# Layer 0 of a graph network: lookups, products, gathers and scans moved into one stage

## The chip, the cores and the metric

The kernel runs on one core of a Trainium2 chip. A core has TensorE (PE), VectorE (DVE), ScalarE (ACT), GpSimd (POOL) and SyncE (SP); each takes its instructions in order and they wait for each other on semaphores. The metric is the time of one execution on the device in microseconds (us), the median of several; lower is better.

## The reference

3125 nodes of 768 features pass through a two-layer graph attention network (GAT) and a mixture-of-experts network. Only layer 0 of the GAT is touched:

```python
h = (x @ W).reshape(n, heads, out_c)             # x layer-normed; 8 heads of 96
al_s = einsum('nhc,hc->nh', h, a_src)
al_d = einsum('nhc,hc->nh', h, a_dst)
e = leaky_relu(al_s[src] + al_d[dst], 0.2)       # 50000 edges, sorted by dst
m = segment_max(e, dst)
ex = exp(e - m[dst])
z = segment_sum(ex, dst)
out = segment_sum(h[src] * (ex / z[dst])[:, :, None], dst) + bias
```

## The kernel before

Nodes are padded to 25 blocks of 128 (`NB`), edges to 392 tiles of 128 (`NT`). The program is a row of parts, `run(setup)`, `run(features)`, `run(transform)`, `run(scores)`, `run(aggregate)`, and then layer 1 (`features_next`, `products_scores`, ...) and the experts. Each part has a block of its own; the next begins when all engines have finished it. Within a part the order on each engine is the order of the code.

`features` (L284) first makes the attention weights `wa` (12 pairs of a product and a reduction on VectorE, L256 and L257), then handles the 25 blocks: statistics and normalising on VectorE (L331 to L340), six transposes (L352) and six small matmuls for the scores (L360) on TensorE, the square root and two copies (L385, L387) on ScalarE. It ends by storing the table `score_tab`.

`transform` (L533) has 28 turns of 14 edge tiles. Of each turn, 6 tiles' source scores are looked up on TensorE: the low seven bits of `src` are broadcast by a matmul (L653), compared with the partition number (`picks`, L756), the one-hot picks rows of the table by matmul (`lookup`, L662; the table stands in three bf16 parts), and VectorE masks the block and sums (`masked`, L761 to L770). The other 8 tiles are gathered by GpSimd from `score_tab` (L722), up to four turns ahead (`AHEAD`), by indices that VectorE copies to `islot` (L775). Each turn also counts, for the node of each edge, with one-hots of `dst` (`hots`, L792, and L670); the counts give each node's first edge, `first_idx`. The first 25 turns each carry the products of one block (L679, one accumulator), whose rows ScalarE copies and stores to `feat_tab`. The first 12 turns carry the weights of layer 1 as well.

`scores` (L895) scatters each node's `al_d` to the place of its first edge (25 indirect DMAs, L909), reads that array back, and scans: a forward maximum, a backward maximum and the spread of the first values. Each is eight scans, a carry through TensorE, and eight scans again (L955, L966, L968). Five passes over 3136 elements, the exponential, a trip through memory and 32 transposes (L934) give the edge weights.

`products_scores` of layer 1 (L984) does all this for one head in one stage; there every score is looked up, in groups of 8 tiles with the low bits read back from memory (`lo_rows`), and GpSimd has the scatters alone (L1032).

## Time and profile before

| | |
|---|---|
| median of 3 runs | 2875.5 us (2863.57 to 2877.48) |
| the profiled execution's own time | 2895.24 us |
| its span in the trace | 2893.3 us |
| mean granted clock of TensorE | 0.764 |
| busy: TensorE, VectorE, ScalarE, GpSimd | 62%, 45%, 28%, 45% |
| `features` ends, `transform` ends, `scores` ends | 111.5, 523, 629.8 us |

The rows below are of that one execution. L679 is line 679 of the kernel before. A row of a timeline gives the start and the length in us, the engine, the line, the operation with what it writes and reads, and in brackets how long the engine was idle before it and whose work ended the wait; "issue" means that the profile shows nothing it waited for. A row of a group gives the busy time, the mean length in ns, and the idle time before its instructions.

### The profile page before, as it was taken

To read this page: it belongs to the slowest core of one execution; us is meant where nothing else is said; L and a number is where in the kernel's file an instruction comes from. 1 tells how busy PE (TensorE), PEld (TensorE's weight loads), DVE (VectorE), ACT (ScalarE), POOL (GpSimd) and SP (SyncE) were. 2 spreads that over 40 slices of the span, in tenths; PEclk is the share of its full clock that TensorE was granted. 3 is DMA by queue.
4 is the path that set the end of the run, shared out by engine and by line. 5 is a ranking of instruction groups with operands and counts; after the bars stand their busy time and mean duration, and the time that the engine had idled before them with its cause. 6 is when DMAs were issued, how large, how long until landed. Compare 5 with 4: busy or idle time off the path is not lost. (4 is left out here: it accounts for less than half of the span.)

```text
span 2893.3 us, 47710 instructions
## 1 busy us (share of the span) xinstructions
PE 1802.4 (62%) x15107; PEld 1191.7 (41%) x15108; DVE 1307.3 (45%) x2560; ACT 797.7 (28%) x2189; POOL 1309.7 (45%) x1277
## 2 busy tenths in 40 slices
PE   3678888125645555566567955555555568899970
PEld 2445554013333333334334533333333346677750
DVE  7646655655655566548367124111111125311116
ACT  3301111013323333344222323333333332233320
POOL 0266755426767676760221136666666610111216
PEclk9789889556666766758789976676676677899995
DMA  4311111037777787765389698999889874344559
GB/s 142 106 35 41 37 35 30 24 106 248 253 238 251 250 253 252 253 209 176 92 215 261 177 258 288 314 310 316 307 311 317 307 255 150 110 164 156 165 170 400
DMA packets 178077, 577.27 MB, mean 200 GB/s; under 512 B 40579, under 2 KB 49794, under 8 KB 177752
## 3 DMA queue, kind: packets, MB, share of 16 engines
q0 software_dynamic: 88208, 373.59, 42.2%
q1 hardware_dynamic: 64462, 133.66, 13.6%
q10 hardware_dynamic: 25344, 69.32, 6.2%
q8 instruction: 23, 0.38, 0.1%
q14 instruction: 40, 0.33, 0.0%
HBM read 473.58 MB, written 96.45 MB: 197 GB/s over the span
## 5 line engine op out<-in xcount | busy, mean ns | idle before, releaser
L722 POOL DMA_INDIRECT work<-score_tab,islot x224 | 235.3, 1050 | 143.7 <-DVE islot L775 75.8
L1314 POOL DMA_INDIRECT ring<-feat_tab,islot x196 | 234.9, 1198 | 88.3 <-issue 51.6
L1378 PE MATMUL acc<-ring,work 128*32 128x192 f32 x1952 | 179.6, 479 | 127.2 <-issue 67.4
L1572 PE MATMUL acc<-ring,work 128*32 128x192 f32 (+1 forms) x1952 | 171.3, 477 | 139.4 <-issue 106.8
L679 PE MATMUL acc<-wg,work 128*128 128x384 f32 x600 | 227.9, 529 | 28.7 <-issue 24.7
L1494 POOL DMA_INDIRECT ring<-feat_tab,src_t x196 | 195.7, 998 | 108.8 <-PE acc L1572 54.0
L1120 PE MATMUL acc<-wg,work 128*128 128x384 f32 x600 | 215.7, 509 | 19.2 <-ACT work L1177 19.2
L1351 DVE TENSOR_TENSOR ring<-ring,edges 128x768 f32<-128x768 f32 x196 | 185.3, 960 | 89.6 <-DMA ring<-feat_tab,islot 76.8
L1382 PEld LDWEIGHTS acc<-edges,work 128*32 128x32 f32 x982 | 148.2, 152 | 100.9 <-issue 4.7
L679 PEld LDWEIGHTS acc<-wg,work 128*128 128x128 f32 x600 | 120.6, 206 | 122.1 <-issue 59.7
L1572 PEld LDWEIGHTS acc<-ring,work 128*32 128x32 f32 x1952 | 87.3, 144 | 202.3 <-issue 179.9
L1378 PE MATMUL acc<-work 128*32 128x192 f32 x1104 | 99.0, 438 | 106.6 <-ACT work L1436 49.4
L2019 POOL COPY tile_idx<-wg 128x3 int32 x19 | 4.6, 244 | 338.4 <-PE tps L2032 224.5
L1314 POOL DMA_INDIRECT work<-feat_tab,islot x112 | 127.9, 1142 | 56.0 <-issue 27.2
L1572 PE MATMUL acc<-work 128*32 128x192 f32 x1104 | 100.4, 484 | 81.0 <-issue 69.9
L1120 PEld LDWEIGHTS acc<-wg,work 128*128 128x128 f32 x600 | 113.6, 197 | 87.4 <-ACT work L1177 19.3
L1440 ACT ACTIVATE work<-work 32x192 f32<-32x192 f32 x400 | 143.8, 360 | 5.3
L1650 ACT ACTIVATE work<-work 32x192 f32<-32x192 f32 x400 | 143.8, 359 | 5.3
L1494 POOL DMA_INDIRECT work<-feat_tab,src_t x112 | 108.2, 966 | 62.3 <-PE acc L1572 31.1
L2140 DVE TENSOR_TENSOR edges<-acc,wg 128x192 f32<-128x192 f32 x57 | 20.4, 358 | 251.8 <-PE acc L2040 235.7
L1382 PE MATMUL acc<-edges,work 128*32 x982 | 122.7, 198 | 2.3 <-issue 2.2
L2040 PE MATMUL acc<-big,work 128*128 x684 | 122.1, 329 | 1.0 <-ACT work L2096 1.0
(383 smaller groups left out, 3742.2 us busy)
## 6 DMA issues: line engine op xcount, KB each, us to landing
slot_out<-ring SPq DMA_DIRECT2D x57, 384.0 KB
feat_tab<-work ACTq DMA_DIRECT2D x50, 384.0 KB
ring<-lo_rows SPq DMA_DIRECT2D x49, 256.0 KB, 5.8
edges<-in_w_slow SPq DMA_DIRECT2D x28, 384.0 KB, 9.9
edges<-in_w_hebb POOLq DMA_DIRECT2D x28, 384.0 KB, 7.9
edges<-in_w_fast POOLq DMA_DIRECT2D x28, 384.0 KB, 9.4
unit_sum<-edges SPq DMA_DIRECT2D x28, 384.0 KB, 7.0
agg_raw<-work ACTq DMA_DIRECT2D x25, 388.0 KB
```

What stands on the lines that cost most here:

```text
L679: m = nc.tensor.matmul(acc[:, sl * 2 + c, 0:C // 2], xT[sl][:, k, :], wg[:, k, c * (C // 2):(c + 1) * (C // 2)], start=(k == 0), stop=(k = ...
L722: pool.indirect_dma_start(sg[:, h, k * H:(k + 1) * H], None, score_tab[0], bass.IndirectOffsetOnAxis(ap=islot[:, h * 8 + k:h * 8 + k + 1], ...
L1120: m = nc.tensor.matmul(acc[:, sl * 2 + c, 0:C // 2], xT[sl][:, k, :], wg[:, k, c * (C // 2):(c + 1) * (C // 2)], start=(k == 0), stop=(k = ...
L1314: pool.indirect_dma_start(rows[k][:, 0:C], None, feat_tab[l], bass.IndirectOffsetOnAxis(ap=islot[:, h * UN + k:h * UN + k + 1], axis=0)).t ...
L1351: V.tensor_tensor(r3, r3, ex[:, ds(i * UN + k, 1), :].rearrange("p a h -> p h a").to_broadcast([P, H, C // H]), ALU.mult).then_inc(msg_rea ...
L1378: m = nc.tensor.matmul(sums_ps[c * WIN:(c + 1) * WIN, 0:CHUNK], hot, row[:, c * CHUNK:(c + 1) * CHUNK], start=start, stop=True, skip_group ...
L1382: return nc.tensor.matmul(sums_ps[0:WIN, CHUNK:CHUNK + ZC], hot, ex[:, ds(t, 1), :].rearrange("p a h -> p (a h)"), start=False, stop=True, ...
L1440: nc.scalar.activation(raw[sl][w * WIN:(w + 1) * WIN, c * CHUNK:(c + 1) * CHUNK], stage[w % 2][c * WIN:(c + 1) * WIN, 0:CHUNK], ACT.Copy)
L1494: pool.indirect_dma_start(rows[k][:, 0:C], None, feat_tab[1], bass.IndirectOffsetOnAxis(ap=src_t[:, t:t + 1], axis=0)).then_inc(row_in[k], 16)
L1572: m = nc.tensor.matmul(sums_ps[c * WIN:(c + 1) * WIN, 0:n], hot, row[:, c * CHUNK:c * CHUNK + n], start=start, stop=True, skip_group_check ...
L1650: nc.scalar.activation(raw[b % 2][w * WIN:(w + 1) * WIN, c * CHUNK:(c + 1) * CHUNK], stage[w % 2][c * WIN:(c + 1) * WIN, 0:CHUNK], ACT.Copy)
L2040: m = nc.tensor.matmul(acc[:, 2, 0:HID], xTs[k][:, c, :], big[:, ds(e * HID + c * EH, HID)], start=(c == 0), stop=(c == KC - 1))
```

## The change

`features` is written out over the blocks. x is loaded ahead of W0; VectorE starts the statistics at once and makes `wa` in blocks 3 to 8; ScalarE normalises (with a new `shift`), and one copy of the transposed block instead of two is made. The index work of `transform` moves here. A node's first edge is now found so: the last edge's `dst` of each tile (`dst_last`) is counted per node, which gives the tile in which the node's edges begin (`tiles_of_nodes`); GpSimd gathers that tile's row of `dst_rows` for each node (25 gathers), and VectorE compares it with the node's number (`compared`).

`products_scores_first` takes the place of `transform` and `scores`. It has the form of layer 1's stage: 56 groups of 4 tiles (224 tiles) are looked up on TensorE, four groups between the product chunks of a block, two accumulators; GpSimd sends the 25 scatters and then gathers 168 tiles, with a wait for the lookups at every eighth; the scan of the first values comes after group 48, the two others after the last gather; products of the last blocks stand between.

```diff
+GF = 4
+FIRST_GROUPS = (LOOK_BLOCKS + 2) * GPB
+LOOKED = FIRST_GROUPS * GF
+PACE = 8
...
+                    def compared(g):
+
+                        dve.wait_ge(near_in[g], 16 * SB)
+                        for j in range(SB):
+                            b = g * SB + j
+                            V.tensor_scalar(less[:, j, :], near[:, b, :].bitcast(i32), node_f[:, b:b + 1], None, ALU.is_lt)
+                            ins = V.tensor_scalar(same[:, j, :], near[:, b, :].bitcast(i32), node_f[:, b:b + 1], None, ALU.is_equal)
+                        st.step(ins)
+                        V.tensor_reduce(below_n[:, g * SB:(g + 1) * SB], less, AX, ALU.add)
+                        st.step(V.tensor_reduce(miss[:, g * SB:(g + 1) * SB], same, AX, ALU.max))
...
+                    for b in range(NB):
+                        statistics(b)
+                        if b > 0:
+                            shifts(b - 1)
...
+                        if 3 <= b < 3 + KC:
+                            for j in range(2):
+                                attention_weights(st, 0, b - 3, j, wg[:, b - 3, :], a_vec[j], wa_tmp)
...
+                @block.gpsimd
+                def _(pool):
...
+                    for b in range(NB):
+                        pool.indirect_dma_start(first_val[0], bass.IndirectOffsetOnAxis(ap=first_idx[:, b:b + 1], axis=0),
+                                                al_node[:, b, H:2 * H], None, bounds_check=EP - 1,
+                                                oob_is_err=False).then_inc(first_st, 16)
+                    for t in range(LOOKED, NT):
+                        n = t - LOOKED
+                        if n % PACE == 0:
+                            pool.wait_ge(look_ps, max(1, n * FIRST_GROUPS // (NT - LOOKED) - 2))
+                        pool.indirect_dma_start(src_s[:, t, :], None, score_tab[0],
+                                                bass.IndirectOffsetOnAxis(ap=src_p[:, t:t + 1], axis=0)).then_inc(gather_in, 16)
...
+                    def lookup(G, j):
+                        pe.wait_ge(pick_ready, G + 1)
+                        pe.wait_ge(look_used, G + 1)
+                        for c in range(GF):
+                            for part in range(3):
+                                m = nc.tensor.matmul(look[j][:, c // 2, (c % 2) * W:(c % 2 + 1) * W],
+                                                     pick[j][:, c * P:(c + 1) * P], table[:, part, :],
+                                                     start=(part == 0), stop=(part == 2))
+                        m.then_inc(look_ps, 1)
...
+                    steps = {(LOOK_BLOCKS, 5): lambda: carry_out(0, dst_s[:, NT - 1, :]),
+                             (LOOK_BLOCKS + 1, 1): lambda: carry_back(0, 2),
+                             (FB + 1, 0): lambda: carry_out(1, peak[:, NT - 1, :]),
+                             (FB + 1, 1): lambda: carry_back(1, 0),
+                             (FB + 3, 1): lambda: carry_out(2, top[:, 0, :]),
+                             (FB + 3, 2): lambda: carry_back(2, 1),
+                             (NB - 1, 0): lambda: weights_out(0),
...
+                    with dve.Fori(0, KC // 2) as i:
+                        st.loop(i, 2 * (LO * 3 + 4))
+                        for s in range(2):
+                            for g in range(LO):
+                                picks((i * 2 + s) * LO + (g + 1), (g + 1) % 2, (g + 1) % LO, i * 2 + (s + (g + 1) // LO))
+                                masked((i * 2 + s) * LO + g, g % 2)
+                            next_attention(i * 2 + s, s, i)
+                    st.done(KC // 2)
...
+                    dve.wait_ge(first_in, 16)
+                    whole_scan(0, 2, dst_s, first_s, keep, held, False, 0.0)
+                    for G in range(KC * LO, FIRST_GROUPS):
+                        if G + 1 < FIRST_GROUPS:
+                            picks(G + 1, (G + 1) % 2, (G + 1) % LO, (G + 1) // LO)
+                        masked(G, G % 2)
+                    dve.wait_ge(gather_in, 16 * (NT - LOOKED))
+                    whole_scan(1, 0, peak, src_s, rst_f, most, False, NEG)
+                    whole_scan(2, 1, top, peak, rst_b, most, True, NEG)
...
         run(setup)
         run(features)
-        run(transform)
-        run(scores)
+        run(products_scores_first)
         run(aggregate)
```

## Rows read from the trace of the kernel before

**Rows 1.** Busy time by stage (us, instructions), then granted clock, DMA share, GB/s.
```profile
111.50:523.00 411.50, 311.87 (x1674) 192.96 (x1674) 248.15 (x361) 40.20 (x75) 237.87 (x230) 0.84 0.17 42
523.00:629.80 106.80, 8.49 (x38) 5.77 (x38) 62.56 (x60) 10.60 (x10) 32.06 (x25) 0.50 0.14 46
```

**Rows 2.** Waits in 140 to 520: total us, times, longest.
```profile
POOL work L722 <- DVE islot L775: 66.9, 10, 11.7
DVE edges L766 <- remote: 60.6, 12, 14.8
```

**Rows 3.** Timeline, gathers of `transform`: start, length, instruction, idle before.
```profile
122.25 1.09 POOL L722 DMA_INDIRECT work<-score_tab,islot  x1 [8.85 <-DVE islot L775]
...
491.40 0.95 POOL L722 DMA_INDIRECT work<-score_tab,islot  x1 [0.30 <-issue]
```

**Rows 4.** Timeline, ScalarE's slot copies, one a turn.
```profile
186.17 0.84 ACT L617 ACTIVATE work<-big 128x768 f32 x1 [29.31 <-PE acc L679]
...
336.77 0.84 ACT L617 ACTIVATE work<-big 128x768 f32 x1 [8.57 <-PE acc L679]
...
366.75 0.84 ACT L617 ACTIVATE work<-big 128x768 f32 x1 [28.38 <-remote]
```

**Rows 5.** Timeline, `products_scores` of layer 1 during its scatters.
```profile
1437.51 0.85 DVE L1245 TENSOR_TENSOR edges<-tps,edges 128x300 f32<-128x300 f32 x2 [7.66 <-DMA big<-feat_tab,islot]
...
1454.48 0.97 POOL L1032 DMA_INDIRECT first_val<-al_node,first_idx  x1 [0.31 <-issue]
...
1459.30 0.85 DVE L1245 TENSOR_TENSOR edges<-mps,edges 128x300 f32<-128x300 f32 x2 [18.98 <-DMA big<-feat_tab,islot]
```

**Rows 6.** Timeline, `features` and the head of `transform`.
```profile
15.44 0.96 DVE L256 TENSOR_TENSOR edges<-wg,edges 128x768 f32<-128x768 f32 x1 [15.30 <-DMA edges<-in_a_dst]
...
39.31 0.56 DVE L331 BATCH_NORM_STATS2 stats<-ring 128x6 f32<-128x384 f32 x1
...
98.03 0.68 DVE L340 TENSOR_SCALAR work<-ring,carry 128x768 f32<-128x768 f32 x1
...
107.24 0.39 SPq L313 DMA_DIRECT2D score_tab<-al_node  x1
...
111.50 0.33 DVE L736 CAST edges<-al_node 128x200 bf16<-128x200 f32 x1 [12.79 <-PEq L300]
...
121.40 0.36 DVE L798 TENSOR_SCALAR keep<-keep 128x392 int32<-128x392 int32 x1
...
130.72 0.35 DVE L828 TENSOR_SCALAR edges<-edges 128x392 int32<-128x392 int32 x1
```

**Rows 7.** Groups of VectorE in `transform`: busy us, mean ns, idle before.
```profile
L770 DVE TENSOR_REDUCE edges<-edges 128x1200 f32 (+1 forms) x28 | 39.3, 1403 | 6.4 <-DVE edges L766 4.7 <-issue 1.5
...
L766 DVE TENSOR_TENSOR edges<-acc,edges 128x400 f32<-128x400 f32 x56 | 32.2, 575 | 47.5 <-remote 35.9 <-DVE edges L766 6.3 <-PE acc L662 2.6
```

**Rows 8.** Timeline, one group of lookups in layer 1's `products_scores`.
```profile
1582.51 0.48 DVE L1236 TENSOR_SCALAR edges<-ring,edges 128x1024 bf16<-128x1024 bf16 x1 [0.18 <-DVE edges L1250]
...
1583.51 0.85 DVE L1245 TENSOR_TENSOR edges<-mps,edges 128x300 f32<-128x300 f32 x2 [0.23 <-PE tps L1109]
...
1585.55 0.49 DVE L1236 TENSOR_SCALAR edges<-ring,edges 128x1024 bf16<-128x1024 bf16 x1 [0.18 <-DVE edges L1250]
```

**Rows 9.** Timeline, the second half of `scores`.
```profile
571.65 7.04 DVE L955 TENSOR_TENSOR_SCAN edges<-keep,edges 128x392 f32<-128x392 f32 x8 [16.34 <-DMA edges<-first_val]
...
587.74 3.42 DVE L975 TENSOR_TENSOR edges<-edges 128x3136 f32<-128x3136 f32 x1
...
621.21 0.43 PE L934 MATMUL tps<-ident,ring 98*128 98x98 f32 x1 [41.26 <-DMA ring<-edge_ex]
...
629.77 0.17 DVE L1336 COPY islot<-src_t 128x14 int32<-128x14 int32 x1 [24.77 <-PEq L905]
```

**Rows 10.** The page's group of the products.
```profile
L679 PE MATMUL acc<-wg,work 128*128 128x384 f32 x600 | 227.9, 529 | 28.7 <-issue 24.7
```

**Rows 11.** Timeline, one of the products' weight loads.
```profile
256.82 0.34 PEld L679 LDWEIGHTS acc<-wg,work 128*128 128x128 f32 x1 [0.30 <-issue]
```

850 lines of the change are left out of this document (417 added, 433 removed).

## The prediction

> **What bounds the kernel now.** I read three things in this order: the busy time by stage, who waited for whom inside the first of the touched stages, and then single instructions at the stage borders. The stages `transform` and `scores` take 411.5 and 106.8 us, 518.3 together; with `features` (to 111.5) that is 629.8 us of the span of 2893.3 [rows 1]. No engine is full in either: in `transform` TensorE is busy 312 of 411.5 us at a granted clock of 0.84, VectorE 248, GpSimd 238; in `scores` VectorE is busy 62.6 of 106.8 and TensorE 8.5 [rows 1]. So the second stage is a chain on one engine, and the first is something that holds three engines together.
>
> What holds them shows in the waits. GpSimd waited 66.9 us for `islot`, which VectorE fills after each turn, and VectorE waited 60.6 us in `masked` for a releaser that the profile calls "remote", which is none of the engines' finished work [rows 2]. GpSimd's own pace is 0.95 + 0.30 = 1.25 us a gather, so 224 gathers need 280 us; from the first at 122.25 to the end of the last at 492.35 it took 370 [rows 3]. 90 us were lost, 0.40 us a gather. Much of it sits in a few stretches: one turn on ScalarE, at best some 10 us (8.57 of them idle), lasted from 336.77 to 366.75, 30 us, and one like it ended at 186.17 [rows 4]. Layer 1 shows the same without gathers: in `products_scores` VectorE stood 7.66 and 18.98 us before two multiplications while GpSimd sent its 25 scatters, and went on at 1459.30, after the last scatter at 1454.48 [rows 5]. I call this the standstill: engines with long instruction streams stop while GpSimd sends small indirect DMAs back to back, and go on when it pauses. Why, the trace doesn't say.
>
> **The change, part by part.** I place S, the start of the new stage (before: 111.5), then T, when VectorE has all scores of sources, then the tail.
>
> *features, to S.* Before, VectorE first made the attention weights, 15.44 to 39.31, 23.9 us, and only then the first statistics; 25 blocks follow to 98.03, 2.35 us each, and the score table is stored at 107.24 [rows 6]. After, x comes first, so statistics can begin near 7 us (the first load is issued a little after 4 us; my guess from the store-to-next-stage distance of 107.24 to 111.50, which bounds a small DMA and a stage border by 4.3 us [rows 6]). But VectorE gets much more. The normalising (0.68 us) goes to ScalarE, which drops its second copy of each block for it; with the new shift (0.15) what is left is about 1.8 us a block, 45 us for 25. Added: weights 23.9; what was the head of `transform`, 121.40 to 130.72, 9.3 us [rows 6]; `compared`, 5 groups of ten 128-wide comparisons and two reductions over 640, by the reduction's rate (1.403 us for 1200, [rows 7]) 0.75 each and 0.2 a comparison (one of 392 elements takes 0.36 [rows 6]), 3.5 to 3.7 us a group, 18.4; histogram, small copies and index sums, 6. Sum 7 + 45 + 23.9 + 9.3 + 18.4 + 6 = 110, plus some 5 us of waits for W0, which now stands behind nine loads in SP's queue and is wanted at block 3. Then the last block runs through the pipeline (normalise, six transposes, copy, six matmuls, two copies) in about 5 us (before 9.2, 98.03 to 107.24, with three blocks under way), and 4.3 to the next stage as before. S = 124; 118 if the waits vanish, 134 if 25 new gathers of rows in this stage cost 0.40 us each as above. The stage gets 12 us longer.
>
> *Lookups, S to T, on VectorE.* Removed: the counting one-hots, the broadcast through PSUM, the index copies and the waits for gathers. Left are 56 groups of 4 tiles. Layer 1 does the same with 8 narrower tiles: 1582.51 to 1585.55, 3.04 us a group [rows 8]. Here the pick has 512 instead of 1024 elements (less 0.2), the mask 100 instead of 200 (less 0.1), the multiplications are two of 400 instead of 300 (0.575 and 0.50 pipelined against 0.85, plus 0.2 [rows 7, 8]), the reduction has 800 instead of 600 (0.95 by the rate above, plus 0.2). 3.15 us, and 56 of them 176. The weights of layer 1, the same 12 pairs as in `features`, 24. The first-value scan, now between groups 48 and 49, 571.65 to 587.74 before, 16.1 [rows 9]. Start 4. Sum 220.
>
> *Gathers, on GpSimd.* 25 scatters and 168 gathers at 1.25 to 1.28: 247, 251 with start and landing. This is longer than 220, so without the standstill T = S + 251, and VectorE has 31 us to spare. With it VectorE's time grows. The scatters meet the first lookups as in layer 1: 7.66 + 18.98 = 27 us [rows 5]. The gathers: 90 x 168/224 = 67 if the price of before holds, 0 at best. Against 67 speaks the new wait: at every eighth gather GpSimd stops until the lookups are near, where before it could run four turns (32 gathers) ahead. The two longest stretches of before, about 20 us each too long (both in [rows 4]), could then not last. (90 - 40) x 168/224 = 37. I take 27 + 37: T = S + 284, and GpSimd, held by the same checks, ends beside it. Behind the checks nothing else waits on GpSimd's queue.
>
> TensorE: 12 products a block, 0.529 us each in the mean of before [rows 10], and 48 small matmuls, about 11 us against 14.8 on VectorE (four groups and half a pair of weights). It is no bound at this clock; at 1.2 GHz throughout, with 0.64 a product [rows 11] and the small ones twice as long, it would be about 17, 2 us a block over VectorE, some 20 us more at most. The double accumulators take ScalarE's copy off its path, worth nothing here.
>
> *Tail from T.* Two scans of 16.1; each carry now stands behind product chunks in TensorE's order, 2 us in all. The five passes, the exponential, and its way out to memory and back, 587.74 to 621.21, 33.5 [rows 9]. Then the transposes: before 8.5 us to the next stage, at 629.77 [rows 9]. Now six sit between the twelve products of the last block, which at the lower clock (1.2 GHz) come every 0.30 + 0.34 us [rows 11], 7.7, and that block's store must land: 8.5 + 7.7 + 2. Sum 32.2 + 2 + 33.5 + 18.2 = 86; 75 if the products hide. Where the 106.8 us of `scores` went: 32.4 of them, the wait for the scatters (16.34) and the scan of first values, are now inside S to T [rows 9].
>
> **Sum.** 124 + 284 + 86 = 494 against 629.8: 136 us less. Profiled execution 2895.2 (span 2893.3) gives 2759. The median shown, 2875.5, lies 19.7 below the profiled one; I subtract from it: 2740. Later stages get the same tables and indices and should keep their lengths.
>
> **A rule weighed.** VectorE's picks are bf16 from SBUF to SBUF; in layer 1 they take 0.48 us for 1024 elements, twice what one element a cycle of the 1200-wide reduction gives [rows 7, 8], while the scatters beside them stay at 0.97 [rows 5]. The Trainium skill (SBUF — State Buffer, Who interferes with whom) says that such `tensor_scalar` modes take the port pair that GpSimd shares, and the other side blocks fully. By that rule GpSimd would lose at most 56 x 0.24 = 13 us, an estimate of mine; GpSimd's 251 would become 264, still under 284. The rows here show no such loss.
>
> A second rule gives a rival of its own: the Trainium skill (Runtime: NRT & Kernel Launch, Instruction fetch mechanics) says that a taken branch outside the fetched window stalls its engine.
>
> **Rivals.**
> - *No standstill*, chance 0.22: the loops, not the indirect DMAs, cause it, and they shrink (TensorE's from 27 turns to 6, VectorE's from 6 to 3, ScalarE's from 12 to none). For: gathers stayed at 0.95 during it. Against: layer 1 stood in mid-body, and as long as the scatters ran [rows 5]. T = S + 251, 33 less than forecast: 2707. This is also what the rule just named would give.
> - *Full price*, 0.22: pauses don't help. 27 + 67: T = S + 314: 2770.
> - *The other side*, 0.04: between two checks the engines stand entirely and lookups advance only in the pauses. 21 checks x 8 x 1.25 = 210 us instead of 37: 2740 + 173 = 2913, slower. For: that one turn of 30 us [rows 4]. Against: the gathers of 28 turns took 370 us, 13.2 a turn [rows 3], so most went beside running engines. It decides from 173 us lost in the gathers up, 8 us a check.
> - *features is the surprise*, 0.04: VectorE's order there stalls on SP's queue or the near gathers; 30 us more, 2770.
>
> **Chances.** Forecast 0.48. Its own range 2715 to 2765. Of the range I leave out the far side and a small rest: 2707 less 30 for a short tail and S = 118 gives 2677; 2770 plus 10 for S = 134 and 15 to 20 for the lower clock 2795 to 2800. So 2675 to 2800. A measurement of this kernel tells some 0.5%, 14 us. Faster 0.93, same 0.03, slower 0.04.
>
> **What would show it.** Right: score table stored near 120; 56 groups about 3.15 us apart where GpSimd pauses; VectorE gaps of some 27 us within the first 35 us of the stage; gathers ending within 10 us of the last lookup; the five passes ending near 460; `aggregate` starting near 494. Wrong: `features` over 135; VectorE waiting long for the last gathers (no standstill); a period above 5 us a group; or the last block's products starting after the transposes and adding more than 10 us.

## The result, and the profile after

The changed kernel takes 2801.2 us (median of 4 runs, 2798.4 to 2805.7) against 2869.5 for the kernel before beside it (2862.3 to 2877.5): a ratio of 0.9763, 95% interval 0.9727 to 0.9798. That is 68 us faster. The forecast was 136 faster, 2740, with a range to 2800: the direction held, the size was halved, and the time lies just outside the range.

The three stages, in the view of busy time by window of the changed kernel (columns as in [rows 1]; the cuts are the start of the new stage, the first scan over the source scores, and the first instruction of `aggregate`):

```profile
0.00:145.44 145.44, 74.16 (x491) 57.10 (x492) 93.53 (x286) 53.37 (x102) 30.93 (x53) 0.97 0.39 126
145.44:480.73 335.29, 225.91 (x1067) 144.95 (x1068) 185.77 (x330) 29.04 (x50) 189.92 (x194) 0.81 0.23 57
480.73:563.72 82.99, 73.58 (x244) 43.48 (x242) 47.40 (x42) 24.57 (x35) 0.00 (x0) 0.98 0.22 82
```

S is 145.4 (forecast 124), S to T 335.3 (284), the tail 83.0 (86). The three stages end at 563.7 against 629.8 [rows 1], 66 us less. A second profile of the kernel before (below) has them end at 627.7. What follows takes 2232.9 us after and 2232.1 in that second profile, so the change left it alone; the profile on which the forecast stood had 2263.5 there and was 30 us long in stages that the change doesn't touch. The forecast's stages were 69.7 us short. It carried 10.9 us of the other sign from that profile: those 30.6 us too many in the later stages, against 19.7 that it took off for the median. With 2.8 us between the new profiled execution and its median that gives the miss of 61 us. By stage it is +21.4 in S, +51.3 from S to T and -3.0 in the tail.

**features.** The timeline of the changed kernel, TensorE, VectorE and the DMA queue of SyncE, first the steady blocks, then the end:

```profile
85.26 2.78 PE L544 MATMUL tps<-big,wa 128*16 128x128 f32 x24 [1.14 <-ACT edges L602]
...
90.20 2.78 PE L544 MATMUL tps<-big,wa 128*16 128x128 f32 x24 [1.14 <-ACT edges L602]
...
95.15 2.78 PE L544 MATMUL tps<-big,wa 128*16 128x128 f32 x24 [1.14 <-ACT edges L602]
...
99.08 0.26 DVE L522 COPY dst_open<-mps 128x100 f32<-128x100 f32 x1 [9.48 <-PE mps L571]
...
128.22 0.16 DVE L415 SCALAR_TENSOR_TENSOR carry<-carry 128x1 f32<-128x1 f32 x1
...
140.62 0.38 SPq L369 DMA_DIRECT2D score_tab<-al_node  x1
...
145.44 0.33 DVE L942 CAST edges<-al_node 128x200 bf16<-128x200 f32 x1 [16.52 <-PEq L337]
```

Three blocks start their node scores 4.94 and 4.95 us apart, each after 1.14 us idle for L602, ScalarE's copy of scores. VectorE itself, which would need less, stood 9.48 us for a transpose that TensorE had queued behind them, and made its last `shift` at 128.2, where the forecast's sum has it at some 115. From its last `shift` to the store of the score table it took 12.4 us, not 5.

**The standstill.** TensorE, GpSimd and VectorE at the head of the new stage:

```profile
166.78 0.95 PE L834 MATMUL mps<-edges 128*128 128x200 bf16 x9 [0.75 <-DVE edges L955]
168.69 0.25 PE L834 MATMUL mps<-edges 128*128 128x200 bf16 x1 [0.96 <-issue]
170.79 0.25 PE L834 MATMUL mps<-edges 128*128 128x200 bf16 x1 [1.85 <-issue]
...
174.99 0.80 PE L846 MATMUL acc<-wg,work 128*128 128x384 f32 x1 [1.77 <-issue]
177.79 0.80 PE L846 MATMUL acc<-wg,work 128*128 128x384 f32 x1 [2.00 <-issue]
...
176.36 0.97 POOL L789 DMA_INDIRECT first_val<-al_node,first_idx  x1 [0.30 <-issue]
...
178.91 1.00 POOL L796 DMA_INDIRECT edges<-score_tab,src_p  x1 [0.30 <-issue]
...
204.51 1.05 DVE L964 TENSOR_TENSOR edges<-tps,edges 128x400 f32<-128x400 f32 x2 [37.62 <-remote]
```

TensorE has no wait that the profile can name, and yet gets one lookup matmul each 2.1 us and then one product each 1.4 to 2.8 us, while GpSimd sends its scatters and, from 178.91, 16 gathers without a pause. VectorE stands 37.62 us for that one group of lookups ("remote" is again a releaser that the profile cannot name). Its waits of this kind over the stage, and GpSimd's for the lookups:

```profile
DVE edges L964 <- remote: 90.7, 15, 37.6
...
POOL edges L796 <- PE tps L834: 56.1, 7, 20.6
```

**Undisturbed groups and the tail**, in VectorE's and TensorE's timeline:

```profile
401.48 0.35 DVE L955 TENSOR_SCALAR edges<-ring,edges 128x512 bf16<-128x512 bf16 x1 [0.18 <-DVE edges L969]
...
404.70 0.35 DVE L955 TENSOR_SCALAR edges<-ring,edges 128x512 bf16<-128x512 bf16 x1 [0.18 <-DVE edges L969]
...
480.73 7.04 DVE L992 TENSOR_TENSOR_SCAN edges<-rst_f,edges 128x392 f32<-128x392 f32 x8
...
547.95 0.92 PE L869 MATMUL tps<-ident,ring 98*128 98x98 f32 x4 [4.35 <-DMA ring<-edge_ex]
...
563.72 0.17 DVE L1379 COPY islot<-src_t 128x14 int32<-128x14 int32 x1 [31.76 <-PEq L783]
```

A group takes 3.22 us where nothing disturbs it. At T there is no wait for the last gathers (480.73 follows the last group at once), and the six transposes stand between products, as drawn in the forecast.

### The profile page after: what moved, and what is told of

The parts are those of the page before. It is cut to its first block and busy times, and to the rows that moved or that the text cites. A ratio compares the mean times of both kernels' runs of the same rounds, so it can differ in the third digit from the quotient of the medians.

```text
span 2796.6 us, 46260 instructions
## 1 busy us (share of the span) xinstructions
PE 1790.1 (64%) x14721; PEld 1192.4 (43%) x14722; DVE 1246.9 (45%) x2621; ACT 807.3 (29%) x2189; POOL 1255.4 (45%) x1248
## 5 line engine op out<-in xcount | busy, mean ns | idle before, releaser
L1163 PE MATMUL acc<-wg,work 128*128 128x384 f32 x600 | 215.3, 508 | 21.4 <-ACT work L1220 18.7
L796 POOL DMA_INDIRECT edges<-score_tab,src_p x168 | 165.2, 983 | 127.2 <-PE tps L834 56.1
L1615 PEld LDWEIGHTS acc<-ring,work 128*32 128x32 f32 x1952 | 89.7, 149 | 180.3 <-issue 165.4
L2062 POOL COPY tile_idx<-wg 128x3 int32 x19 | 3.9, 207 | 335.3 <-PE tps L2075 221.1
L1615 PE MATMUL acc<-work 128*32 128x192 f32 x1104 | 96.2, 462 | 87.1 <-issue 54.7
L1421 PEld LDWEIGHTS acc<-ring,work 128*32 128x32 f32 x1952 | 58.0, 135 | 173.7 <-issue 156.7
```

The source lines that it names most:

```text
L796: pool.indirect_dma_start(src_s[:, t, :], None, score_tab[0], bass.IndirectOffsetOnAxis(ap=src_p[:, t:t + 1], axis=0)).then_inc(gather_in, 16)
L1163: m = nc.tensor.matmul(acc[:, sl * 2 + c, 0:C // 2], xT[sl][:, k, :], wg[:, k, c * (C // 2):(c + 1) * (C // 2)], start=(k == 0), stop=(k = ...
L1421: m = nc.tensor.matmul(sums_ps[c * WIN:(c + 1) * WIN, 0:CHUNK], hot, row[:, c * CHUNK:(c + 1) * CHUNK], start=start, stop=True, skip_group ...
L1615: m = nc.tensor.matmul(sums_ps[c * WIN:(c + 1) * WIN, 0:n], hot, row[:, c * CHUNK:c * CHUNK + n], start=start, stop=True, skip_group_check ...
```

## The experiments

The runs were made in seven groups, each on one chip and with the kernel before beside them; in the table, rows with the same time of the kernel before are one group. The groups are of two kinds: in four the kernel before takes 2868 to 2904 us, in three 2602 to 2608. I call them the slow and the quick chip, but only for short: the record numbers the chips of six groups, and number 9 stands for a slow group (the b-runs) and for a quick one (e2 and e3). So what makes the difference need not be the chip itself. The changed kernel's first run was in a slow group. All edits are to the changed kernel. The changed kernel itself was run in two groups only, both slow, with stretches of 335.3 and 337.7 us; kernels of other groups are compared with these.

| run | chip (before) | ratio, 95% interval | S | S to T |
|---|---|---|---|---|
| changed kernel | 2869.5 | 0.9763, 0.9727 to 0.9798 | 145.4 | 335.3 |
| a1_no_small | 2608.0 | 0.9687, 0.9637 to 0.9736 | 144.5 | 240.2 |
| a2_no_scatters | 2608.0 | 0.9655, 0.9618 to 0.9692 | 144.6 | 243.4 |
| a3_straight | 2608.0 | 0.9747, 0.9695 to 0.9799 | 145.2 | 255.4 |
| a4_copy_first | 2608.0 | 0.9716, 0.9678 to 0.9754 | 133.8 | 256.9 |
| b2_kernel_changed | 2868.4 | 0.9763, 0.9735 to 0.9791 | 144.2 | 337.7 |
| b3_combined | 2868.4 | 0.9689, 0.9665 to 0.9713 | 134.2 | 322.4 |
| b4_no_small_again | 2868.4 | 0.9434, 0.9407 to 0.9460 | 143.3 | 239.9 |
| c1_no_scatters_again | 2891.4 | 0.9659, 0.9631 to 0.9688 | 144.1 | 305.4 |
| c2_straight_again | 2891.4 | 0.9724, 0.9692 to 0.9756 | 145.5 | 329.3 |
| c3_paced | 2891.4 | 0.9744, 0.9717 to 0.9772 | 142.8 | 324.1 |
| c4_combined_64 | 2891.4 | 0.9715, 0.9676 to 0.9754 | 134.5 | 336.7 |
| d1_paced_60 | 2601.6 | 0.9715, 0.9674 to 0.9755 | 133.8 | 255.2 |
| d2_unpaced | 2601.6 | 0.9805, 0.9753 to 0.9858 | 144.4 | 254.7 |
| d3_combined_again | 2601.6 | 0.9683, 0.9645 to 0.9720 | 133.8 | 247.7 |
| e1_unpaced_again | 2903.6 | 1.0202, 1.0159 to 1.0245 | 146.4 | 477.3 |
| e2_paced_60_again | 2603.1 | 0.9698, 0.9648 to 0.9748 | 134.0 | 255.4 |
| e3_paced_60_looser | 2603.1 | 0.9703, 0.9655 to 0.9752 | 132.1 | 253.0 |

### GpSimd's small DMAs left out

```diff
-                    for b in range(NB):
-                        pool.indirect_dma_start(first_val[0], ...)
-                    for t in range(LOOKED, NT):
-                        ...
+                    nc.gpsimd.memset(src_s[:, LOOKED:NT, :], 0.0).then_inc(gather_in, 16)
...
-                            sp.wait_ge(first_st, 16 * NB)
...
-                    dve.wait_ge(gather_in, 16 * (NT - LOOKED))
+                    dve.wait_ge(gather_in, 16)
```

The first run:

> The changed kernel with GpSimd's 25 scatters of first values and 168 gathers of scores left out (the scores of those tiles are set to 0 once, the first values stay 0). Theory A, the standstill comes from GpSimd's small indirect DMAs sent back to back: VectorE's waits of kind remote and issue in its 56 groups (88 us in the changed kernel, the longest 37.6) all but vanish, and the stretch from the new stage's start to the last group shrinks from 335 us to about 56 x 3.2 + 24 + 20 = 223 to 250 us, the kernel from 2801 to about 2700 to 2715 us. Theory B, the engines stop at the taken branches of their own loops or for long instruction streams alone: the waits stay near 80 us, the stretch near 330, the kernel at about 2800. Theory C, the first 37.6 us are the collision of instruction fetches with the stage's opening loads (8 rows of low bits, four of 384 KB): these 37.6 stay and the later 50 go, the kernel is at about 2750.

It fell on a quick chip (2526.6 us), and there nothing could be told apart: the stretch was 240.2 us as theory A says, but the kernels beside it that keep their gathers had no remote wait either. The same kernel on a slow chip:

> The kernel of the first experiment again (no scatters and no gathers on GpSimd in the new stage; those scores are 0). On a chip like that of the first experiment (before at 2608): ratio to the kernel before 0.965 to 0.972 and a stretch of 240 us, as there. On a chip where the kernel before takes 2870: theory A (the standstill is called by GpSimd's small DMAs) says the stretch is 240 to 250 us and the kernel 85 to 95 us under the changed one, at 2705 to 2720; theory B (it comes of loops, of long streams or of that chip's memory alone) says the remote waits stay and the stretch is 300 us or more.

The median was 2708.6 us and the stretch 239.9 against 337.7 in the changed kernel beside it. Not one wait of kind remote is left. VectorE's longest single wait in the stage is now that for the attention vectors, and the longest for TensorE's lookups is small:

```profile
DVE edges L945 <- DMA work<-in_a_dst: 8.1, 1, 8.1
...
DVE edges L954 <- PE tps L824: 1.2, 2, 0.6
```

Theory A is shown for the slow chip: small indirect DMAs on GpSimd's queue cost TensorE and VectorE 98 us of this stage. Theory B falls, since this kernel keeps every loop. So does C, since it keeps the opening loads. The windows 180 to 220 put it side by side. With no small DMAs:

```profile
180.00:220.00 40.00, 30.12 (x163) 20.88 (x162) 31.88 (x55) 3.44 (x6) 0.00 (x0) 0.92 0.23 77
```

and in the changed kernel on the same chip:

```profile
180.00:220.00 40.00, 10.56 (x32) 5.77 (x33) 7.13 (x13) 1.72 (x3) 21.00 (x23) 0.50 0.09 19
```

163 matmuls against 32, and a granted clock of 0.92 (mostly the upper of its two levels, 2.4 GHz) against 0.50 (the lower, 1.2 GHz): TensorE, which had all but stood, was at the lower clock as well.

### The scatters alone

```diff
-                    for b in range(NB):
-                        pool.indirect_dma_start(first_val[0], ...)
...
-                            sp.wait_ge(first_st, 16 * NB)
```

> The changed kernel with only the 25 scatters left out (the first values stay 0); all 168 gathers are sent. Theory A with every small DMA alike: the stretch falls by the scatters' share of the standstill, 25 x 1.27 = 32 us of GpSimd's 200, so the 37.6 us wait shrinks to 5 to 15 us and the kernel is 20 to 33 us faster than the changed one, at about 2770 to 2780. Theory A with the gathers as the cause: the first burst of gathers (16 before the first pause) takes the scatters' place, the wait stays at 25 us or more, kernel at about 2790 to 2800. Theory B (loops or streams alone): nothing changes.

> The changed kernel without the 25 scatters of first values (those stay 0), all 168 gathers sent, meant for a chip like that of the changed kernel's first run (the kernel before at 2870). There the standstill costs 337.7 - 239.9 = 98 us of the stretch with all 193 small DMAs. If each DMA calls its share by its time on GpSimd (scatters 32 of 197 us), the stretch is about 321 and the kernel 2785 to 2792. If the scatters' unbroken run behind the stage's start is what costs (VectorE's first remote wait, 38.3 us), the stretch is about 300 and the kernel 2760 to 2772. If the first 16 gathers take the scatters' place: 330 or more, 2795 to 2805. On a chip where the kernel before takes 2608 nothing new: 243 us and a ratio of 0.966.

On the quick chip the stretch was 243.4 us (2518.4 us in all). On the slow one 305.4, 32 less than with scatters (337.7, from the b-runs, as is the 239.9 below); the first long wait is gone (the longest remote one is 11.9 us), 60.3 us of remote waits remain. That is nearest to the second case: the ratio of 0.9659 would be 2770 us where the kernel before takes 2868. The scatters, first part of the unbroken run behind the stage's start, cost about one for one, 32 us of sending and 32 us of standstill. The 168 gathers alone still cost 305.4 - 239.9 = 65.5 us, 0.39 us each.

### No pause at all

```diff
-                        if n % PACE == 0:
-                            pool.wait_ge(look_ps, max(1, n * FIRST_GROUPS // (NT - LOOKED) - 2))
+                        if n == 0:
+                            pool.wait_ge(look_ps, 1)
```

> The changed kernel with no pause between GpSimd's gathers (one wait for the first group, then 168 in a row after the 25 scatters). If TensorE gets only a matmul or so per 0.7 to 2.1 us while GpSimd sends without a pause, it stands for most of 25 x 1.27 + 168 x 1.25 = 242 us, in which some 60 to 100 matmuls (3 to 5 groups) get through, and 51 groups follow undisturbed at 3.2: a stretch of 242 + 51 x 3.2 + 44 = about 450 us, and a kernel about 110 us slower than the changed one, at 2910 (ratio 1.01 to 1.02) where the kernel before takes 2870 to 2890. If each DMA costs the same 98 / 193 = 0.5 us of standstill whatever the spacing, the stretch is 330 to 345 us and the ratio 0.976. Where the kernel before takes 2608 nothing changes in either.

> The unpaced kernel again (168 gathers in a row behind the 25 scatters), for a chip on which the kernel before takes 2870 to 2890; its first run fell on one with 2602, where the stretch took 254.7 us against the changed kernel's 257 or so and told nothing of the standstill. Price by the unbroken run: a stretch of about 450 us and a ratio of 1.01 to 1.02. Price per DMA whatever the spacing: 330 to 345 us and 0.976.

On the quick chip: 254.7 us, set by GpSimd (VectorE waited 11.7 for the last gather). On the slow chip the same kernel is 2% slower than the kernel before (interval 1.6% to 2.4%), 2964.7 us, and the stretch is 477.3. VectorE's and GpSimd's timeline there:

```profile
219.04 1.06 DVE L964 TENSOR_TENSOR edges<-tps,edges 128x400 f32<-128x400 f32 x2 [50.73 <-remote]
...
263.84 1.06 DVE L964 TENSOR_TENSOR edges<-mps,edges 128x400 f32<-128x400 f32 x2 [41.81 <-remote]
...
319.84 1.06 DVE L964 TENSOR_TENSOR edges<-tps,edges 128x400 f32<-128x400 f32 x2 [53.01 <-remote]
...
364.67 1.06 DVE L964 TENSOR_TENSOR edges<-mps,edges 128x400 f32<-128x400 f32 x2 [41.84 <-issue]
...
415.79 1.06 DVE L964 TENSOR_TENSOR edges<-tps,edges 128x400 f32<-128x400 f32 x2 [48.09 <-remote]
...
391.13 0.94 POOL L796 DMA_INDIRECT edges<-score_tab,src_p  x1 [0.30 <-issue]
```

One group of lookups each 45 to 56 us, until the last gather has been sent at 392.1. In the windows:

```profile
220.00:260.00 40.00, 6.01 (x16) 2.60 (x16) 1.60 (x4) 0.00 (x0) 30.25 (x33) 0.50 0.08 7
...
440.00:480.00 40.00, 34.96 (x200) 24.40 (x199) 31.74 (x59) 3.75 (x7) 0.00 (x0) 0.96 0.34 106
```

16 matmuls in 40 us while GpSimd sends, 200 after, the clock 0.50 and then 0.96. GpSimd sent for 244 us and the stretch grew by 477.3 - 239.9 = 237: at full length of run the engines all but stand. The number of DMAs is that of the changed kernel, which lost 98. So the price is not one per DMA; it hangs on the pauses.

### Paced from the first one

```diff
                     for b in range(NB):
+                        if b % 3 == 0:
+                            pool.wait_ge(look_ps, b // 3 + 1)
...
-                        if n % PACE == 0:
-                            pool.wait_ge(look_ps, max(1, n * FIRST_GROUPS // (NT - LOOKED) - 2))
+                        if n % 4 == 0:
+                            pool.wait_ge(look_ps, 9 + n * (FIRST_GROUPS - 9) // (NT - LOOKED))
```

> The changed kernel with all 193 small DMAs of GpSimd tied to the lookups from the first one on: one wait for the next group before every third scatter and before every fourth gather, so that GpSimd is never more than one group ahead (in the changed kernel it sends 25 scatters and 16 gathers without a pause). GpSimd's own time then gives at least 3.8 us a group for the first nine and 3.5 us for the other 47, so 200 to 205 us plus 24 + 20 + 9, at least about 255. If unbroken runs cause the standstill and a short pause lets the streams in, the first remote wait of 38.3 us goes to under 8 and the stretch falls from 337.7 to 270 to 310 us, the kernel to 2740 to 2775 where the kernel before takes 2870. If each DMA costs its share whatever the spacing, the stretch stays within 10 us of 337.7 or grows. On a chip where the kernel before takes 2608 there is no standstill to save: the stretch goes from 257 to 260 to 270, ratio 0.977 to 0.98.

The longest remote wait fell from 38.3 to 8.2 us, and the time to the end of group 48 and the weights from 290.5 to 262.9 us, but the whole stretch only to 324.1, 14 us less where 28 to 68 had been forecast. It fits neither case, and in the kernel's time the gain is not clear of the noise (0.9744 against 0.9763, the intervals overlap). The end shows why:

```profile
427.45 0.94 POOL L798 DMA_INDIRECT edges<-score_tab,src_p  x1 [24.41 <-PE tps L836]
...
444.66 1.06 DVE L966 TENSOR_TENSOR edges<-mps,edges 128x400 f32<-128x400 f32 x2 [5.66 <-remote]
...
461.94 1.06 DVE L966 TENSOR_TENSOR edges<-tps,edges 128x400 f32<-128x400 f32 x2 [8.21 <-remote]
```

GpSimd, tied to the lookups, stood through the scans of first values; then it sent its last gathers nearly in a row, and the last eight groups had the waits of 5.66 and 8.21 us. Up to group 48 this kernel still lost 68 us against the one without small DMAs (262.9 against 195.1, there 143.3 to 338.4): short pauses take off some of the price, not most. The schedule that spreads the gathers better, in the combined kernel:

```diff
-                        if n % PACE == 0: ...
+                        if n < 100 and n % 3 == 0:
+                            pool.wait_ge(look_ps, 9 + n * 39 // 100)
+                        if n >= 120 and n % 3 == 0:
+                            pool.wait_ge(look_ps, 48 + (n - 120) * 3 // 8)
```

> The combined kernel (scores' copy first, moved wait, 60 groups, 152 gathers) with GpSimd's DMAs paced from the first one on: a wait for one more group before every third scatter, then before every third of the first 100 gathers (so that they spread over groups 9 to 48), no wait for the next 20 (they go while VectorE makes the scans of first values), and again one for every third of the last 32. In the kernel paced before, the time to the end of group 48 fell by 27.6 us against the changed kernel, and 14 us were given back in the last 8 groups, where GpSimd, held still for 24.4 us during the scans, sent 32 gathers in a row. If unbroken runs set the price, this kernel keeps both: against the combined one's 322.4 us a stretch of 295 to 310, and a ratio to the kernel before of 0.958 to 0.966 where that takes 2870 to 2890. If each DMA sets it: within 0.003 of the combined one's ratio (0.969).

> The paced kernel with 60 groups again, for a chip on which the kernel before takes 2870 to 2900. The unpaced kernel has shown that the price goes by the unbroken run. If short pauses from the first DMA on then save what is left of the first run (a first wait of 16.7 and one of 23.6 us in the combined kernel), the stretch is 295 to 312 against the combined one's 322.4, and the ratio 0.958 to 0.966. If the streams need more than a short pause, the stretch is within 8 us of 322 and the ratio 0.967 to 0.972.

> The same with each wait of a gather one group earlier (two groups in the last 32), so that the gathers end some 5 us sooner. Where the kernel before takes 2870 to 2900: if a tighter tie to the lookups is what feeds the streams, 2 to 8 us slower than the tight one; if the end of the gathers holds the scans, 2 to 7 us faster. Where it takes 2602 (no standstill): the wait for the gathers of 7.7 us falls to 3 or so, and the kernel comes within 5 us of the combined one.

All three were in quick groups, where there is nothing to win back: stretches of 255.2, 255.4 and, looser by a group, 253.0, against 247.7 for the combined kernel. They cost 5 to 8 us there; what they would give on a slow chip stays open.

### The loops written out

```diff
-                    with pe.Fori(0, LOOK_BLOCKS // 2) as i:
+                    for i in range(LOOK_BLOCKS // 2):
...
-                    with dve.Fori(0, KC // 2) as i:
+                    for i in range(KC // 2):
```

> The changed kernel with the two loops of the new stage written out: TensorE's 6 turns over the first 12 blocks and VectorE's 3 turns over the first 48 groups become straight instruction streams; nothing else is changed. Theory B (the stops come from taken branches outside the fetched window): the 88 us of VectorE's waits of kind remote shrink to under 20 and the kernel comes to about 2730. Theory A: the streams only grow, so at least as much has to be fetched while GpSimd sends its DMAs: waits of 80 to 120 us, kernel at 2795 to 2835.

> The changed kernel with TensorE's and VectorE's loops of the new stage written out. On a chip where the kernel before takes 2870: if the loops' turns (taken branches) share in the standstill of 98 us, it falls by more than 15 us (2785 or less); if the streams starve as any stream does while GpSimd sends, nothing changes within 8 us (2795 to 2812); if code already run in a loop is spared the fetch, the straight streams cost more, 10 to 40 us (2812 to 2845). On a chip where the kernel before takes 2608: a ratio of 0.975 as before.

On the slow chip VectorE's remote waits are 84.1 us (87.1 in the changed kernel), the longest 36.4, and the stretch 329.3 against 337.7; the ratios' intervals overlap. TensorE's and VectorE's loops are no cause of the standstill; a gain of a few us from writing them out can be neither shown nor excluded. On the quick chip the same kernel has a stretch of 255.4 us and takes 2547.0.

### features: ScalarE's copy first

```diff
                     for b in range(NB + 2):
+                        for q in range(scored(b - 4), scored(b - 3)):
+                            scores_out(q)
                         if b < NB:
                             root(b)
...
-                        for q in range(scored(b - 4), scored(b - 3)):
-                            scores_out(q)
```

> The changed kernel with one edit in the features stage: ScalarE copies the node scores of the block before (scores_out) at the head of its turn and no longer at its end, behind the square root, the normalise and the copy of the transposes. Theory D, TensorE's second node_scores of a block stands behind ScalarE's whole turn, so a block takes 4.95 us: the period falls to about 4 us, the score table is stored at about 125 to 132 and no longer at 140.6, and the kernel is 8 to 15 us faster, at about 2787 to 2793. Rival E, TensorE's own work (transposes and 12 matmuls of a block) or VectorE's statistics set the period: the store stays within 3 us of 140.6 and the time within 0.2 per cent of the changed kernel's.

```profile
75.16 2.78 PE L544 MATMUL tps<-big,wa 128*16 128x128 f32 x24
...
78.90 2.79 PE L544 MATMUL tps<-big,wa 128*16 128x128 f32 x24
...
82.88 2.78 PE L544 MATMUL tps<-big,wa 128*16 128x128 f32 x24
...
90.56 0.26 DVE L522 COPY dst_open<-mps 128x100 f32<-128x100 f32 x1 [2.13 <-PE mps L571]
...
128.97 0.38 SPq L369 DMA_DIRECT2D score_tab<-al_node  x1
...
390.65 4.44 DVE L992 TENSOR_TENSOR_SCAN edges<-rst_f,edges 128x392 f32<-128x392 f32 x5 [15.52 <-DMA edges<-score_tab,src_p]
```

This timeline is of the quick chip. The node scores of two blocks start 3.74 and 3.98 us apart, VectorE waits 2.13 us and not 9.48 for its copy, the store comes at 129.0, and S is 133.8. All seven kernels with this edit, on either chip, have S at 132.1 to 134.5, all without it at 142.8 to 146.4; within one group it gives 8 to 11 us. Theory D holds. Between 75 and 93 us TensorE now has next to no wait, so what sets the period is its own work, 0.87 us for the transposes, 2.78 for the scores and 0.29 for turning them back. The kernel takes 2534.9 us; the ratio's interval overlaps that of the kernel with straight loops beside it, so in the whole time the 11 us are not shown by themselves. The last line shows the bound of the next stage on the quick chip: GpSimd's own 193 DMAs end 15.5 us after VectorE is ready.

### The kernel before and the changed one, again, and a combination

> The kernel before, profiled again beside the next three runs. The first four experiments ran on a chip where the kernel before took 2608 us, not 2870, and where waits of kind remote are all but missing. Theory F, the standstill belongs to that first chip and not to the kernel's streams: where this profile's span is near 2610, VectorE's 12 waits of kind remote for its own lookups (60.6 us in all) and ScalarE's remote waits at its product chunk (141.8 us) are under 10 us in all, and the second part of the first layer (411.5 us from 111.5 to 523) is 40 to 70 us shorter; where the span is near 2890, all of them are there again. Rival: they are there at either span.

> The changed kernel itself on the same chip as the runs beside it. If the kernel before takes about 2610 here: 2540 to 2550, with the stretch from the new stage's start to the last source score at 255 to 260 us (set by GpSimd's 25 scatters and 168 gathers, about 251 us), and no remote wait over 5 us. If it takes about 2870 here: 2795 to 2805, the stretch at 325 to 345 us and a first remote wait of 30 to 45 us.

The group was a slow one: 2861.7 us (one execution) and 2804.8. The kernel before showed its remote waits again, 110.4 us at ScalarE's copy (L617) and 47.7 at L766, as theory F says for that span. It was never profiled on a quick chip, so what it lost there is not known.

```diff
-FB = LOOK_BLOCKS + 4
+FB = LOOK_BLOCKS + 5
-FIRST_GROUPS = (LOOK_BLOCKS + 2) * GPB
+FIRST_GROUPS = (LOOK_BLOCKS + 3) * GPB
...
                     def next_attention(k, s, n):
+                        dve.wait_ge(vec_in, 32)
                         dve.wait_ge(chunk_in[s], n * 16 + 16)
...
-                    dve.wait_ge(vec_in, 32)
```

and the copy first.

> The changed kernel with three edits: ScalarE's copy of the node scores at the head of its turn, 60 groups of four tiles on TensorE and not 56 (152 gathers, not 168), and VectorE's wait for the attention vectors moved from before its loop into the first use of them. Where gathers set the end (a chip on which the kernel before takes 2610): the first edit gives 11.6 us, 16 gathers fewer 15.7, of which VectorE's 4 groups more (12.9 us, less the 9 us of the moved wait) leave some 12, so about 20 to 24 us less than the changed kernel, at 2520 to 2525. Where the standstill sets it (before at 2870): 11.6 us, and of 16 gathers' standstill some 4 to 8 back against 12.9 us of groups: 8 to 20 us less, at 2780 to 2793.

> The combined kernel again, on the same chip as the paced one: a ratio of 0.967 to 0.971 where the kernel before takes 2870 to 2890, with a stretch of about 322 us; about 0.967 where it takes 2608, with a stretch of about 247.

> The combined kernel (copy of the scores first, moved wait for the vectors) with 64 groups on TensorE and 136 gathers in place of 60 and 152. VectorE gets 4 x 3.2 = 12.9 us more. Where the kernel before takes 2870: the step from 56 to 60 groups took 15.3 us off the stretch, 9 of it by the moved wait, so 16 gathers are worth about 19 us of standstill; if the next 16 are worth as much, the stretch falls by 6 us more to about 316 and the kernel to 2775; if the standstill was already under the other waits, it grows by up to 13 us, to 2795. Where the kernel before takes 2608: VectorE alone sets the end, some 10 us over the combined kernel with 60 groups, at 2530 to 2535.

60 groups and 152 gathers: 2781.9 us, 0.9689 on the slow chip and 0.9683 on the quick one, the lowest ratio on either of the kernels that send all their DMAs. On the slow chip it is 23 us under the changed kernel beside it, and their intervals don't overlap; on the quick chip it is not clear of its neighbours. 64 groups, run in another slow group, seem to lose it again (336.7 against 322.4, while four groups cost 12.9; 0.9715 against 0.9689, the intervals overlap): the second 16 gathers fewer gave nothing back that these runs show.

## Why the prediction missed, by its steps

- **S: 145.4, forecast 124; 21 us.** The sum of VectorE's work was sound. What failed is "Then the last block runs through the pipeline (...) in about 5 us", and the idea behind it that VectorE sets the pace. TensorE and ScalarE did: ScalarE's copies of scores stood behind its square root, normalise and copy of transposes, two node scores a block waited for them, and TensorE's queue held up VectorE (9.48 us). The edit took about 11 of the 21 away. The other 10 can be read from its trace: some 7 us are the node scores left over after the last block (the store comes 11.7 us after the last `shift`, forecast 5) and some 3 VectorE's own sum (last `shift` at 117.3).
- **S to T, VectorE's 220: measured 239.9.** Its groups in the kernel without small DMAs, by line (busy us, mean ns, idle before):

```profile
L959 DVE TENSOR_REDUCE edges<-edges 128x800 f32 (+1 forms) x56 | 55.2, 986 | 12.6 <-DVE edges L954 11.5
...
L262 DVE TENSOR_TENSOR edges<-work 128x768 f32<-128x768 f32 x12 | 11.5, 959 | 1.5 <-DVE edges L959 1.3
L263 DVE TENSOR_REDUCE wa<-edges 128x768 f32 x12 | 11.4, 953 | 1.7
```

  With the masks the 56 groups take some 182 us, forecast 176; the weights 26 (24); the first-value scan 20.2 (16.1), its carry 4.5 us behind product chunks, which I had counted for the two scans of the tail and not for this one; and 8.1 us go to the wait for the attention vectors, ahead of the loop, which I had not seen.
- **The scatters' 27 and the gathers' 37: 98 in all, 64 forecast.** The step that failed is the discount: "(90 - 40) x 168/224 = 37. I take 27 + 37". I argued that a wait at every eighth gather rules out long stretches. The runs without scatters put the gathers at 65.5 us, not 37, which is 0.39 us each and so the price of before (0.40), and the scatters at 32, not 27. And the first waits don't hold (the first two ask for one group, the third for three), so 25 scatters and 16 gathers went as one run of about 52 us: 37.6 us of standstill at once. The full price of the trace of before, 27 + 67 = 94, was within 4 us. The rival of that name had the right size, but not the right reason: "pauses don't help" is refuted by the kernel without pauses, in which the same DMAs cost 237 us. That the size held is luck, as far as the runs tell: GpSimd's long pauses happened to be alike, 66.9 us for `islot` before [rows 2] and 56.1 + 21.1 us after (for lookups, and of kind remote). Its 2770 lacked the 21 and the 20 us above.
- **GpSimd alone, 251.** Right: 254.7 where the gathers run unpaced and nothing stands; VectorE waited 11.7 us for it.
- **The tail, 86.** 83.0; right.
- **"The other side"**, engines that stand entirely, was called a chance of 0.04. It did not come about over the changed kernel's stage, only in its first run of DMAs; without pauses it does on a slow chip: 2964.7 us, slower than before.
- **The two rules.** What the Trainium skill (SBUF — State Buffer, Who interferes with whom) says of the picks, that they and GpSimd hold each other up, does show in the trace, but small. With no small DMAs all 56 picks take 0.35 us; in the unpaced kernel on the quick chip eight of 56 take 0.46 to 0.56 us, and the gathers that meet a pick near their start up to 1.10 us instead of 0.94. Gathers beside the products of the attention weights (L262) and beside the scans lengthen more, to 1.72 us:

```profile
206.64 0.56 DVE L955 TENSOR_SCALAR edges<-ring,edges 128x512 bf16<-128x512 bf16 x1 [0.18 <-DVE edges L969]
...
245.63 1.72 POOL L796 DMA_INDIRECT edges<-score_tab,src_p  x1 [0.30 <-issue]
```

  The 168 gathers take 166.1 us together there and 158.6 where VectorE stands (the same kernel on the slow chip). So all of it is 7.5 us of GpSimd's time, of which about 1 falls beside picks; the forecast's estimate was 13. (Its reading of the picks in layer 1 was off as well: 0.48 us for 1024 elements is 2.5 times the reduction's rate, not twice.) The rule of the Trainium skill (Runtime: NRT & Kernel Launch, Instruction fetch mechanics) on taken branches does not account for the standstill, which stays without the loops.
- **The sign** came of what was removed: the counting, broadcast and second stage of before, worth 136 by the forecast, remained gone; the three sizes above (21 for S, 20 for VectorE, 31 to 34 for the standstill) ate half.

Shown is that the small DMAs cause the standstill and that it depends on pauses and on the kind of group. What the engines lack meanwhile is open. My expectations took it to be instructions that could not be fetched in time, because matmuls come singly where the profile shows nothing that they waited for. The profile's view of DMAs speaks against that. It lists the two queues that load instructions, and between 147 and 206 us of the changed kernel, where the first standstill begins and ends, neither moves a packet; nor does either between 239 and 392 us of the unpaced kernel on the slow chip, where TensorE ran 55 matmuls one by one:

```profile
239.00:392.00 153.00, 23.59 (x55) 9.52 (x54) 7.75 (x15) 1.72 (x3) 113.66 (x121) 0.50 0.08 8
```

Over its whole stretch that kernel has nine such packets on the slow chip and nine on the quick one. So these matmuls did not wait for instructions to land one after the other; whether something else slows their issue no run tells. Why a slow chip does this and a quick one doesn't stays open too, and so does whether the number of DMAs or the 128 small rows of each is what counts: both were always left out or spaced together.

## What to carry to other kernels

Count the small indirect DMAs that GpSimd sends in one unbroken run beside engines with long streams, and price the run at its full length until a trace shows less; break up the first run too, since a margin in a pacing wait is no pause. When an engine's turn serves two pipelines, try the copy that another engine waits for at the head of the turn; here it gave 8 to 11 us. Compare stretches only between runs with the same kernel beside them, since the two kinds of group differ by more than any edit here. And profile the kernel before twice: one execution here was 30 us long in stages that nobody touched.

## What the runs showed of the hardware

- The same program's time differs by 10% between groups of runs: the kernel before took 2602 to 2608 us in three and 2868 to 2904 in four. The slow kind is not slower throughout. The kernel without small DMAs ends its first three stages at 467.3 us on the slow chip and at 468.9 on the quick one. What is longer there is both `aggregate` stages (665.2 us against 599.2, and 628.3 against 529.6) and `products_scores` of layer 1 (303.0 against 287.6); in all three GpSimd sends indirect DMAs beside the other engines' streams, in the `aggregate` stages rows of 768 values. The other stages are within 1 us of each other. The second `aggregate` and the experts to the end, on the slow chip:

```profile
1536.30:2164.60 628.30, 338.12 (x4136) 211.38 (x4136) 152.61 (x322) 213.16 (x725) 387.57 (x394) 0.64 0.87 303
2287.10:2705.20 418.10, 316.68 (x1596) 245.43 (x1596) 110.64 (x278) 111.07 (x228) 115.24 (x126) 0.89 0.56 201
```

  and on the quick one:

```profile
1456.90:1986.50 529.60, 317.94 (x4136) 150.65 (x4136) 152.28 (x322) 213.67 (x725) 387.99 (x394) 0.71 0.96 360
2108.40:2527.30 418.90, 316.17 (x1596) 245.10 (x1596) 110.67 (x278) 111.07 (x228) 115.15 (x126) 0.89 0.57 201
```

  The 303 GB/s against 360 are the same work in a longer time; in the last stages both move 201 GB/s. So the standstill goes with the kind of group, and a memory that is slower for everything is not what the traces show.
- A run of 25 indirect DMAs need not hurt. In `features` GpSimd sent its 25 gathers without a pause, from 12.9 us on, and VectorE was busy 35.25 of the 40 us from 15 to 55 on the slow chip and 35.16 on the quick one; S is 144.2 and 144.5 us. Only TensorE stood on the slow chip, 12.7 us in two waits, and it had little to do there.
- On the slow chip a run of small indirect DMAs beside lookups and products (each 0.95 us and 0.30 us between them) leaves TensorE about one matmul in 1.4 to 2.8 us, and all but stops it if the run lasts: 244 us of sending cost 237. On the quick chip the same kernel loses nothing, and GpSimd's own time is the bound.
- The ratios hardly differ between the chips (combined 0.9689 and 0.9683), though what sets T differs: the standstill on one; on the other GpSimd's queue in the kernels with 168 gathers, and VectorE's own work in the combined one, which starts its last scans without a wait for the gathers.
